# Writing masked key copies with ScalarE instead of four SBUF-to-SBUF transfers, in the first layer of a two-layer gated attention kernel

## The reference

```python
x = x + tanh(g_xattn[0]) * attention(layernorm(x), ctx)   # 16 heads of 8, mask by chunks of 32
x = x + tanh(g_ffn[0]) * moe(layernorm(x))                # 8 experts, top 1, gelu

q = (query @ Wq + bq).reshape(b, s, H, hd)                # H = 16, hd = 8
k = (key @ Wk + bk).reshape(b, s, H, hd)
scores = einsum('bqhd,bkhd->bhqk', q, k) * scale
```

## Time and profile before

| | |
|---|---|
| median of 3 runs | 1628.67 us (1626.63 to 1629.27) |
| the profiled execution | 1626.43 us |
| its span | 1624.7 us |
| mean granted TensorE clock | 0.981 of full speed |
| TensorE busy (matmul) | 93% of the span |
| VectorE, GpSimd, ScalarE busy | 80%, 73%, 65% |

### The profile page before, as it was taken

The page is one execution under the profiler, slowest core; times in us unless marked ns, Lnnn a source line. Parts: engine busy times, 40 slices in busy tenths (PEclk is TensorE's granted clock), DMA queues, the critical chain, the costliest instruction groups (busy, mean ns, idle before and its releaser), DMA issues.

```text
span 1624.7 us, 52801 instructions
## 1 busy us (share of the span) xinstructions
PE 1513.6 (93%) x17129; PEld 1308.8 (81%) x17130; DVE 1293.3 (80%) x4044; ACT 1064.2 (65%) x2661; POOL 1186.9 (73%) x1715
## 2 busy tenths in 40 slices
PE   5899999976999789999999999999999999999996
PEld 4666666755999469888888888888888888889885
DVE  3777778863555378998999889988998999988885
ACT  3777777743556456767766776677667766776664
POOL 4556666642456568888888888888888888888785
PEclk9999999986999999999999999999999999999998
DMA  2322222234553100000000000000000000000000
GB/s 78 110 72 74 78 78 78 78 102 120 147 140 91 29 16 15 20 16 15 21 19 17 15 21 15 21 15 21 15 21 15 17 19 21 15 15 18 5 8 11
DMA packets 92108, 69.05 MB, mean 42 GB/s; under 512 B 13937, under 2 KB 87697, under 8 KB 91921
## 3 DMA queue, kind: packets, MB, share of 16 engines
q1 hardware_dynamic: 76512, 49.34, 10.3%
q0 software_dynamic: 5120, 12.62, 2.4%
q10 hardware_dynamic: 10288, 4.74, 1.1%
HBM read 35.74 MB, written 22.52 MB: 36 GB/s over the span
## 4 chain that ended last, share of the span: by engine, by line
PE 79%; issue 7%; DVE 6%; ACT 3%; DMA 2%; POOL 2%; SPq 1%; POOLq 0%; ACTq 0%; DVEq 0%
PE s_bank L1998 12%; PE s_bank L1999 11%; PE s_bank L2000 11%; PE tb L1815 6%; PE po L1945 4%; PE s_bank L1933 4%; PE s_bank L1795 4%; PE po L1829 3%; PE m L1769 2%; PE s_bank L2146 2%; PE s_bank L1804 2%; ACT pT L889 1%; DVE qkv L1552 1%; DMA kx<-kT 1%; PE s_bank L2133 1%
## 5 line engine op out<-in xcount | busy, mean ns | idle before, releaser
L745 POOL TENSOR_TENSOR qkv<-qkv,scaled 128x384 f32<-128x384 f32 x480 | 489.4, 1020 | 87.2 <-ACT scaled L1020 37.8
L1020 ACT ACTIVATE scaled<-s_bank,wg 128x384 f32<-128x384 f32 x449 | 260.3, 584 | 114.5 <-PE s_bank L2000 109.9
L1998 PE MATMUL s_bank<-proj_hi,hn_hi 128*128 128x384 f32 x900 | 327.0, 363 | 5.6 <-DVE qkv L1552 5.6
L1552 DVE SCALAR_TENSOR_TENSOR qkv<-s_bank,wg,qkv 128x384 f32<-128x384 f32 x449 | 273.9, 610 | 49.8 <-PE s_bank L2000 39.6
L1999 PE MATMUL s_bank<-proj_lo,hn_hi 128*128 128x384 f32 x900 | 302.9, 337 | 0.0
L2000 PE MATMUL s_bank<-proj_hi,hn_lo 128*128 128x384 f32 x900 | 302.2, 336 | 0.0
L889 ACT ACTIVATE pT<-tb 128x512 f32<-128x512 f32 x256 | 152.9, 597 | 136.1 <-PE tb L1815 134.5
L1998 PEld LDWEIGHTS s_bank<-proj_hi,hn_hi 128*128 128x128 f32 x900 | 169.4, 188 | 18.9 <-DVE qkv L1552 14.1
L1815 PE MATMUL tb<-ident,prob 128*128 128x128 f32 x1024 | 161.4, 281 | 15.2 <-ACT pT L889 13.8
L1999 PEld LDWEIGHTS s_bank<-proj_lo,hn_hi 128*128 128x128 f32 x900 | 170.2, 189 | 1.6
L2000 PEld LDWEIGHTS s_bank<-proj_hi,hn_lo 128*128 128x128 f32 x900 | 169.0, 188 | 0.0
(11 more groups left out here) (285 smaller groups left out, 3714.3 us busy)
## 6 DMA issues: line engine op xcount, KB each, us to landing
xs<-sorted_in SPq DMA_DIRECT2D x71, 128.5 KB, 2.1
kx<-kT SPq DMA_DIRECT2D x256, 32.0 KB
sorted_out<-yo SPq DMA_DIRECT2D x71, 64.0 KB, 1.6
xin<-in_x SPq DMA_DIRECT2D x32, 128.0 KB, 2.1
cin<-in_ctx SPq DMA_DIRECT2D x32, 128.0 KB, 2.3
ctx_cols<-xcT SPq DMA_DIRECT2D x32, 128.0 KB, 1.7
w<-in_L_ffn_W SPq DMA_DIRECT2D x16, 256.0 KB, 3.8
xcT<-ctx_cols SPq DMA_DIRECT2D x32, 128.0 KB, 2.8
```

What stands on the lines that cost most here:

```text
L745: g.tensor_tensor(into, into, scaled[m % SCALED][:, 0:cols], ALU.add).then_inc(dense_added, 1)
L1020: ins = act.activation(into, bank[:, 0:3 * D], ACT.Copy, scale=wg[v % 4][:, 1, k:k + 1])
L1552: v.scalar_tensor_tensor(out=acc, in0=bank[:, 0:3 * D], scalar=wg[w % 4][:, 0, k:k + 1], in1=acc, op0=ALU.mult, op1=ALU.add).then_inc(dens ...
L1998: pe.matmul(bank[:, 0:cols], hi[:, tile], of(proj_hi), start=True, stop=False)
```

## The change

In layer one ScalarE writes the four slices of `kx` itself: one activation for each r, over all 128 rows, reading the keys in PSUM, with a per-row scale (1 where p mod 4 is r, else 0) and a per-row bias (that mask times the bias). `kT` and the transfers are used in layer two alone. The products of layer one wait for `k_ready`, which is raised once for each pair of copies. VectorE makes the two small tables `head_mask` and `head_bias` at the start.

```diff
@@ SyncE
-            def place_keys(layer, v):
-                q = s[layer]
+            def place_keys(v):
+                q = s[1]
...
                 if exists(u + 2):
                     store_context(u + 2, par)
-                    place_keys(0, u + 2)
@@ ScalarE
-            act.wait_ge(setup["first_steps"], 3)
+            act.wait_ge(setup["first_steps"], 4)
...
+            def head_keys(v, pair):
+                q = s[0]
+                if exists(v):
+                    act.wait_ge(q["qk_in_psum"], v + 1)
+                    wait(act, q["scores_in_psum"], 4 * v)
+                    for r in (2 * pair, 2 * pair + 1):
+                        ins = act.activation(kx[:, r, :], m1[:, 256:512], ACT.Identity,
+                                             bias=head_bias[:, r:r + 1], scale=head_mask[:, r:r + 1])
+                    ins.then_inc(q["k_ready"], 1)
...
                 queries(0, u + 2)
-                keys(0, u + 2)
+                head_keys(u + 2, 0)
+                head_keys(u + 2, 1)
                 copy_x1T(u - 1)
@@ VectorE
+            v.tensor_reduce(head_mask[:, :], ident[:, :].rearrange("p (m r) -> p r m", r=4), AX_X, ALU.add)
             v.wait_ge(setup["first_steps"], 2)
             v.tensor_copy(bcol[:, :], m1[:, 0:4]).then_inc(setup["first_steps"], 1)
+            v.wait_ge(setup["first_steps"], 3)
+            v.tensor_scalar(head_bias[:, :], head_mask[:, :], bcol[:, 1:2], None, ALU.mult)\
+                .then_inc(setup["first_steps"], 1)
@@ TensorE
-                        wait(pe, q["k_ready"], v)
+                        wait(pe, q["k_ready"], 2 * v)
...
-                    pe.wait_ge(q["keys_placed"], 64 * (v + 1))
+                    if q is s[0]:
+                        pe.wait_ge(q["k_ready"], 2 * v + 2)
+                    else:
+                        pe.wait_ge(q["keys_placed"], 64 * (v + 1))
```

More of the change, by code:

```diff
@@ L162, in flamingo @@
         kx = sb("kx", [P, 4, UNIT])
+        head_mask = sb("head_mask", [P, 4])
+        head_bias = sb("head_bias", [P, 4])
         vb = [sb(f"vb{b}", [P, 4, 8, 2, VW]) for b in range(2)]
@@ L417, in load_unit @@
                 sp.dma_start(cin[par][:, :, :], tokens(a["ctx_1024"], v)).then_inc(ctx_loaded[0][par], 16)
-            def place_keys(layer, v):
-                q = s[layer]
+            def place_keys(v):
+                q = s[1]
                 sp.wait_ge(q["k_ready"], v + 1)
-                if layer == 1 and v == 1:
+                if v == 1:
                     sp.wait_ge(q["scores_in_psum"], 4)
@@ L512, in _ @@
                 load_slot(sl, sl, rows[sl] if sl < 2 else row_of(sl))
-            place_keys(1, 0)
+            place_keys(0)
             slots(sp, slot)
@@ L524, in body1 @@
                 if exists(u + 3):
-                    place_keys(1, u + 3)
+                    place_keys(u + 3)
                 store(u - 2)
             load_context(2)
-            place_keys(1, 1)
+            place_keys(1)
             load_context(3)
-            place_keys(1, 2)
+            place_keys(2)
             load_context(4)
@@ L827, in keys @@
                 if exists(v):
-                    if layer == 1 and v < 2:
+                    if v < 2:
                         act.wait_ge(f["first_keys"], v + 1)
```

## The result

| | before | after |
|---|---|---|
| median of 7 runs | 1629.27 us (1625.40 to 1642.28) | 1644.97 us (1641.38 to 1648.40) |
| the profiled execution, its span | 1626.43, 1624.7 us | 1648.07, 1646.3 us |
| mean granted TensorE clock | 0.981 | 0.969 |

The changed kernel is slower by a small amount that is clear of the noise: ratio 1.0073, with a 95% interval from 1.0041 to 1.0105. (The quotient of the two medians is 1.0096, also inside it.) The forecast was 1644 us, 0.95% slower. The two profiled executions lie 21.6 us apart, the medians 15.7 us. So what is read from the traces explains these two executions, and some 6 us of it differ from run to run.

What follows compares the result with a forecast made beforehand. TensorE bounds stage one (busy 182 of 200 us), its logits waiting on ScalarE's `x1T`. Terms +14.8, +3.5, -0.8, +0.5, 0, -2.6 make +15.4 on 1626.43: 1641.8 us; plus 2.2 to the median, 1644 us (1629 to 1663).

Steps and rivals of the forecast that it cites:

- The place: In a stage-one body, ScalarE's chain into `x1T` ends last before TensorE's logits, so copies put ahead delay them.
- The faster rival: Logits don't wait for `x1T` and copies run in ScalarE's idle time: 1618 us, chance 0.07.
- The price of a copy: Each ScalarE copy with two operands takes 0.45 us; four instead of one add 1.44 us a body ahead of `x1T`.
- What TensorE gets back: The wait ahead of the logits shrinks the "issue" gap in the values' matmuls, returning 0.7 us a body (0 to 0.92).
- the reading of body 1: Body 1 has no gap, logits to mask 2.13 us against 3.05, taken as following from TensorE's earlier wait.
- The late bodies: Five loop bodies with a late third exponential lose 0.7 us each, as their pause may move with the copies: +3.5 us.
- The clock: Without the last products' wait, part of the 1.2 GHz stretch from 340.7 to 351 us is regained: -2.6 us.
- The clock falls: Rival: a wait in every body plus a gap that stays brings 1.2 GHz into the loop, 13 us; 1675 us, chance 0.05.
- the case in which nothing comes back: Rival: the gap is a fixed stall of TensorE's sequencer and stays; +33.5 us, 1662 us, chance 0.17.
- The loop's account: Bodies 3 to 27: +14.8 us for 20 ordinary bodies, +3.5 for five late ones, -0.8 for waits for transfers.
- the ends of stage one: First four bodies with waits for transfers +0.5 us, last two 0, after added copies, removed waits and time given back.
- What is removed: TensorE's waits for transfers, 4.6 + 0.8 + 2.0 = 7.4 us, and 2.6 of clock; DMA load itself worth nothing.

Runs made afterwards that it cites:

- one_copy: Kernel before without transfers, ScalarE writing only one of the four key slices, so three quarters of the keys are left out; 1614.82 us against 1631.11, ratio 0.9898.
- busy: Changed kernel with 20 more unread 128x128 matmuls ahead of TensorE's wait for `x1T` in layer one; 1635.41 us, ratio 1.0037 to the kernel before.
- one_copy_traffic: As one_copy, plus four transfers a body of the same shape, of unused data, that TensorE doesn't wait for; 1619.13 us, ratio 0.9951 to the kernel before.
- staged: Kernel before without transfers; slices written from `kT` in SBUF, two ahead of the values' copies, two behind the second probabilities' copy; 1672.64 us, ratio 1.0248.
- two_copies: Changed kernel with only two of the four key copies, so half the keys are left out; 1616.41 us, ratio 0.9902 to the kernel before.

## Why the prediction was right in its total and wrong in its terms

**The place.** Right. `x1T` was the last thing ahead of the logits; the logits start 0.15 us after it in the changed kernel, and TensorE idles 1.54 us there. The faster rival falls.

**The price of a copy.** Right: 0.45 us forecast, 0.447 measured, so 1.79 us for four and 1.43 us more than the single copy of 0.36. An estimate from the figures of the Trainium skill ("ScalarE: Activation LUTs", What ACT_TABLE_LOAD costs) was 492 ns; this trace shows 45 ns less. For the copy with one pointer operand the estimate was 399 ns, and the trace before shows some 350.

**What TensorE gets back.** I took 0.7 us of at most 0.92. Measured: the whole gap. In most bodies without a dip 3.05 to 3.15 us went down to 2.13 to 2.25, about 0.9 us a body. The step that led there, the reading of body 1, was wrong, and that it pointed the right way is luck: in one_copy that body has no gap either, although TensorE waits for no keys. An undisturbed body rose from 10.11 to 10.59 us, 0.48 us, where the sum had 1.44 - 0.70 = 0.74 (bodies of 10.8). The Trainium skill ("Runtime: NRT & Kernel Launch", Instruction fetch mechanics) has the engine fetch by itself while it executes; by that rule the whole gap came back, and it did. No row shows a fetch, so this agreement doesn't show what the gap is.

**The late bodies.** Wrong in sign. I had put down +3.5 us in case the pause moves along. It was gone, in the changed kernel as in one_copy. In the loop before, the bodies over 10.3 us together took 4.3 us more than at 10.14 us each; 0.8 of that is the one wait for transfers, and all of it was won.

**The clock.** This step failed: "The clock: -2.6". Of the 10.2 us of half clock from 340.7 us on 3.4 us were left, and the last two bodies took 0.7 us less than before. But the wait in every body brought six dips of 3.4 us into the loop, and more at its ends; what they cost in the loop is 10.1 us over 25 bodies by the traces of the change and of busy, about 6 us by the ratios. The argument against it, body 1 with its 1.74 us wait at full clock, was one wait by itself, and what was built is one in each body. The rival *The clock falls* named the mechanism and priced it at 13 us, near what was measured. Its time, 1675 us, was far too high because it put the dips on top of the 33.5 us of the case in which nothing comes back; and it held only 0.05 of the chance.

**The loop's account.** Forecast: 14.8 + 3.5 - 0.8 = +17.5 us. Measured: +17.7 us. With 10.62 us for a body at full clock, the mean of busy, and some 10.14 for an ordinary body before, it is made of 25 x 0.48 = +12.0, -4.4 for the late bodies and the wait, and +10.1 for the dips. The forecast for ordinary bodies and the one for late bodies were too high, and the clock in the loop was put at nothing: that the sums agree to 0.2 us is luck. At the ends of stage one the sum had +0.5 and 0, and +1.4 and -0.7 were measured.

**What is removed.** I counted 7.4 us of waits and 2.6 of clock, 10.0 us. Giving up the transfers alone gained 1.02%, 16.6 us; with the traffic left in and nobody seen waiting for it the gain was 0.49%, 8.0 us. "The transfers' load on the DMA engines is worth nothing by itself" is wrong: 0.53% here, some 8.6 us. It didn't disturb the total, since most of it lies in the gap that the change closes in any case. With the transfers kept the extra copies cost 1.27%; without them, 1.0073 / 0.9898 = 1.0177, or 1.8%. The two parts of the change don't add up, because the gap can be given back only once.

**What stays open.** What the "issue" gap is. The idle time that shows in it is 0.5 to 0.6 us in the loop. It follows bursts of small matmuls, it shrinks or closes when 0.5 us or more are put ahead of them, be it idle or filled with other matmuls, it is missing in bodies 1 and 2 of one_copy without any such delay, and with traffic that nobody is seen to wait for a body grows by some 0.28 us. Nothing in the trace shows what TensorE's sequencer does in that time. Why the third exponential is late in five bodies of the kernel before is open as well: in the same bodies of the loop it isn't in one_copy, nor in one_copy_traffic, where transfers of that shape run. What decides when the clock dips is open too. The waits of staged, 0.9 to 1.4 us in nearly every body and TensorE busy 216.24 of 260 us, brought only two stretches of dips between 62 and 340 us, where the waits of 1.5 us in the changed kernel brought six single ones.

## What to carry to other kernels

Before work goes to an engine with idle time, find the place in its list: here 1.43 us ahead of the instruction that TensorE waits for cost 1.8% against the same kernel without it, the dips of the clock included, and 1.59 us of copies put 1.8 us later cost 2 us in all 25 bodies (249.0 against 247.1). A gap labelled "issue" behind a burst of small matmuls can pay for a delay ahead of it, once; try half of the delay to see how much is free. When a change adds a short wait of TensorE to each turn of a loop, look at the granted clock in the whole loop, and don't judge by one body that waited alone.

## What the runs showed of the hardware

- The granted clock fell to 1.2 GHz for 3.4 us at a time, with 41 to 51 us at full clock between, in a loop where TensorE waited some 1.5 us in each body of 10.6 us and was busy 84% of the time (218.94 of 260). In the same window of one_copy (239.28 of 260) and two_copies (236.22) it was full throughout, and 20 matmuls in the wait kept it full (busy).
- Four SBUF-to-SBUF transfers a body cost 0.53% (0.15 to 0.9%) without a wait for them in the trace, at a DMA share of 0.24 instead of 0.22 (one_copy_traffic against one_copy).
- From SBUF, with a scale for each row and no bias, ScalarE takes 1.59 us for four copies of 128x256, 0.40 us each (166.02 to 167.61); from PSUM with both operands 0.45.
